# A pre-norm attention block with FP8 linear layer: value projection and input transposes mixed into one bank, an input load issued earlier, and a rearranged last half slot

## What is computed

```python
def attn(x, qkv_w, qkv_b, proj_w, proj_b):          # x: (16, 512, 256), 16 heads of 16
    qkv = einsum('bsd,ed->bse', x, qkv_w) + qkv_b
    q, k, v = per head
    a = softmax(einsum('bhqe,bhke->bhqk', q, k) / 4)
    out = einsum('bhqk,bhke->bhqe', a, v)
    return einsum('bsd,ed->bse', merged(out), proj_w) + proj_b
def ffn(x, w8, bias, input_scale, weight_scale):
    xq = clip(x / input_scale, -448, 448).astype(float8_e4m3fn).astype(x.dtype) * input_scale
    return einsum('bsi,oi->bso', xq, w8 * weight_scale) + bias
x = x + attn(layernorm(x), ...)
x = x + ffn(layernorm(x), ...)
```

## Time and profile before

| | |
|---|---|
| median of the runs | 968.55 us |
| the profiled execution | 968.59 us |
| its span, first to last instruction | 966.8 us |
| PE busy | 930.0 us (96%) |
| DVE busy | 843.8 us (87%) |
| ACT busy | 656.4 us (68%) |
| POOL busy | 515.9 us (53%) |
| one slot in the middle | 55.8 us |

### The profile page before, as it was taken

One profiled execution on the slowest core, in us unless ns is written; L12 is line 12 of the kernel. 1 busy time (PEld: TensorE's weight loads), 2 busy tenths in 40 slices (PEclk: granted clock), 3 DMA queues, 4 the chain that ended last, 5 costly groups with the idle time before them and its releaser, 6 DMA issues.

```text
span 966.8 us, 16811 instructions
## 1 busy us (share of the span) xinstructions
PE 930.0 (96%) x5847; PEld 439.4 (45%) x5847; DVE 843.8 (87%) x1264; ACT 656.4 (68%) x1209; POOL 515.9 (53%) x528
## 2 busy tenths in 40 slices
PE   7799999999999999999999999999999999999993
PEld 4343444444444454544444444444444454433342
DVE  5678889898999989898998989899898989989846
ACT  3157777777777777767677776767777776776760
POOL 4522428467373847647383754738285573715222
PEclk9769999999999999999999999999999999999996
DMA  6971635438083554717265472817556280731010
GB/s 174 159 91 44 107 52 99 79 62 138 29 142 53 100 78 77 124 40 140 44 115 64 83 116 50 140 34 128 72 74 105 35 136 10 136 42 35 13 45 23
DMA packets 46350, 79.45 MB, mean 82 GB/s; under 512 B 10104, under 2 KB 13304, under 8 KB 46264
## 3 DMA queue, kind: packets, MB, share of 16 engines
q1 hardware_dynamic: 45976, 77.97, 47.1%
q10 hardware_dynamic: 288, 0.39, 0.3%
HBM read 18.42 MB, written 8.39 MB: 28 GB/s over the span
## 4 chain that ended last, share of the span: by engine, by line
PE 92%; DVE 2%; ACT 2%; SPq 1%; DMA 1%; issue 1%; ACTq 0%; POOL 0%; DVEq 0%; POOLq 0%
PE ps_t L551 29%; PE ps_o L591 26%; PE ps_m L426 10%; PE ps_s L570 8%; PE ps_m L475 5%; PE ps_m L499 5%; PE ps_m L531 3%; PE ps_m L412 1%; ACT pt L709 1%; PE ps_s L483 1%; DMA xin<-in_x 1%; SPq L309 1%; PE ps_m L514 1%; DVE mx L874 0%; PE ps_s L692 0%
## 5 line engine op out<-in xcount | busy, mean ns | idle before, releaser
L709 ACT ACTIVATE pt<-ps_t 128x512 f32<-128x512 f32 x1024 | 558.0, 598 | 213.9 <-PE ps_t L551 210.5
L874 DVE TENSOR_REDUCE mx<-ps_s 128x2 f32<-128x1024 f32 x512 | 615.3, 1209 | 57.4 <-PE ps_s L570 53.7
L551 PE MATMUL ps_t<-qs,ks 50*128 50x512 f32 x1024 | 391.9, 455 | 8.2 <-ACT pt L709 7.9
L570 PE MATMUL ps_s<-ks,qs 48*128 48x512 f32 x1024 | 380.7, 463 | 8.0 <-DVE nmax L923 4.1
L551 PEld LDWEIGHTS ps_t<-qs,ks 50*128 50x128 f32 x1024 | 164.0, 185 | 296.3 <-ACT pt L709 214.0
L591 PE MATMUL ps_o<-pt,vt 128*32 128x512 f32 x2048 | 272.6, 605 | 0.0
L1176 POOL TENSOR_TENSOR on<-ot,rden 128x256 f32<-128x256 f32 x63 | 39.3, 624 | 243.2 <-DVE rden L935 243.2
L570 PEld LDWEIGHTS ps_s<-ks,qs 48*128 48x128 f32 x1024 | 158.4, 188 | 18.9 <-issue 11.8
L426 PE MATMUL ps_m<-xnT_p,wqkv_p 128*128 128x512 f32 x360 | 109.9, 428 | 1.0 <-POOL xnT_p L1145 1.0
L1167 POOL TENSOR_TENSOR parts<-parts 128x512 f32<-128x512 f32 x60 | 81.3, 1356 | 4.9
L591 PEld LDWEIGHTS ps_o<-pt,vt 128*32 128x32 f32 x2048 | 40.4, 108 | 86.1 <-issue 85.1
(11 more groups left out here) (113 smaller groups left out, 763.3 us busy)
## 6 DMA issues: line engine op xcount, KB each, us to landing
qs<-parts SPq DMA_DIRECT2D x186, 128.0 KB, 4.6
ks<-parts SPq DMA_DIRECT2D x186, 128.0 KB, 5.4
xin<-in_x SPq DMA_DIRECT2D x16, 512.0 KB, 3.6
xres<-in_x SPq DMA_DIRECT2D x16, 512.0 KB, 5.8
out<-h SPq DMA_DIRECT2D x31, 256.0 KB, 2.1
qs<-nmax SPq DMA_DIRECT2D x256, 4.0 KB
pt<-in_qkv_wT SPq DMA_DIRECT2D x1, 768.0 KB, 5.2
qs<-parts SPq DMA_DIRECT2D x12, 64.0 KB, 3.6
```

Source lines behind the costliest of these rows:

```text
L551: nc.tensor.matmul(ps_t[:, g, :], ks[par][rows, slot, keys], qs[par][rows, slot, :], start=True, stop=True).then_inc(st_done, 1)
L570: done = nc.tensor.matmul(ps_s[:, s % 2, g, :], qs[par][rows, slot, queries], ks[par][rows, slot, :], start=True, stop=True)
L709: nc.scalar.activation(pt[n % 2][:, w % 2 + 2 * a, w // 2, :], ps_t[:, a, :], ACT.Exp, scale=SCALE).then_inc(exp_done, 1)
L874: dve.tensor_reduce(mx[:, r, :, s % QUARTER], ps_s[:, s % 2, :, :], AX_X, ALU.max).then_inc(max_done, 1)
```

## The change

1. **Mixed blocks.** `VALUES_AND_X = (20, 22, 24, 26)` takes the place of `PROJECT_V` and `TRANSPOSE_X`. Each of the four steps computes a quarter of the value projection (6 matmuls) into one half of `ps_m` and two x transposes into the other half. ACT makes two copies of 128x256 instead of one of 128x512, four times.
2. **Statistics of x earlier** (`LN1_SUM`, `LN1_END`), and POOL's `layernorm_x` ahead of `low_oT(u-2, 0)`.
3. **Early load**: `load(2, 0)` goes to the head of SP's first slot. The x transposes of block 1 go from slot 1 to the end of PE's first slot, behind 5 unread products; the bias product goes to `ps_m`.
4. **Last half slot**: the transposed scores of odd steps go to `ps_s[:, 0, g, :]`, those of even steps stay in `ps_t`, each waiting for the exponentials of two steps before. Fills shrink from 13 to 4. `round_last` goes from step 8 to 6, `ln2_finish` from 3 to 2, `out_back` from 6 to 5; POOL does `layernorm_h` first.
5. **Finish**: both last `values` come ahead of `project_last(0)`; 10 unread products follow it, 30 more follow the last projection.

```diff
-LAST_ROUND = 8
+LAST_ROUND = 6
+LAST_END = 2
+LAST_BACK = 5
+FILL_VALUES = 10
+FILL_NORM = 30
-FILL_STEPS = range(3, 12)
+FILL_STEPS = (2, 4, 6, 8)
-PROJECT_V = (20, 22)
-TRANSPOSE_X = (24, 26)
-TRANSPOSE_X1 = (0, 2)
+VALUES_AND_X = (20, 22, 24, 26)
-LN1_SUM = (7, 12, 13, 15)
-LN1_END = 17
+LN1_SUM = (5, 7, 10, 12)
+LN1_END = 13
+WARM_SCORES = 5
...
+        def t_bank(b, s, g):
+            if b == B - 1 and s > HALF_STEPS and s % 2:
+                return ps_s[:, 0, g, :]
+            return ps_t[:, g, :]
...
             def first_slot():
+                load(2, 0)
                 sp.wait_ge(ones, 1)
...
                 for n in (2, 3):
                     stack(0, 0, n)
-                load(2, 0)
...
-                for half in range(2):
-                    project_v(0, half)
+                for i in range(NJ):
+                    project_values(ps_t[:, i // 2, i % 2 * D:(i % 2 + 1) * D], 0, i)
+                pe.wait_ge(low_ready, 4)
+                for i in range(WARM_SCORES):
+                    nc.tensor.matmul(ps_s[:, 1, 1, :], wqkv_p[:, 0, 0, 0:P], wqkv_p[:, 0, 0, 0:S], start=True, stop=True)
+                for c in range(NC):
+                    transpose_x(1, c)
...
+            def values_and_x(u, i):
+                take_bank("values_and_x", i, u)
+                project_values(ps_m[:, 0:D], u, i)
+                if u < B - 1:
+                    c, half = i // 2, i % 2
+                    pe.wait_ge(xn_ready, u + 2)
+                    for j in range(2):
+                        last = nc.tensor.transpose(ps_m[:, D + j * P:D + (j + 1) * P],
+                                                   xn[:, 2 * half + j, c * P:(c + 1) * P], ident[:])
+                    last.then_inc(xt_done, 1)
...
+                if b == B - 1 and s == HALF_STEPS + 1:
+                    pe.wait_ge(max_done, STEPS * b + STEPS - 1)
+                elif b == B - 1 and s > HALF_STEPS:
+                    pe.wait_ge(exp_done, 2 * STEPS * b + 2 * s + g - 3)
+                elif past(2 * STEPS * b + 2 * s + g - 1):
                     pe.wait_ge(exp_done, 2 * STEPS * b + 2 * s + g - 1)
...
+            def unread(count):
+                for i in range(count):
+                    nc.tensor.matmul(ps_t[:, 1, :], wqkv_p[:, 0, 0, 0:P], wqkv_p[:, 0, 0, 0:S], start=True, stop=True)
...
             def finish(b):
                 values(b, b % 2, UNITS - 1, 0)
+                values(b, b % 2, UNITS - 1, 1)
                 pe.wait_ge(oT_high, NT * b + 1)
-                pe.wait_ge(nmax_split, 8 * b + 8)
                 project_last(0, PAIRS[0:3:2], False)
-                values(b, b % 2, UNITS - 1, 1)
                 pe.wait_ge(oT_low, NT * b + 1)
                 project_last(0, PAIRS[1:2], False)
+                unread(FILL_VALUES)
                 pe.wait_ge(oT_high, NT * b + 2)
                 project_last(1, PAIRS[0:3:2], False)
                 pe.wait_ge(oT_low, NT * b + 2)
                 project_last(1, PAIRS[1:2], True)
+                unread(FILL_NORM)
...
+            def copy_v(b, par, i):
+                act.wait_ge(v_done, NJ * b + i + 1)
+                if b < B - 1:
+                    act.wait_ge(xt_done, 4 * (b + 1) + i + 1)
                 if past(UNITS * (b - 1)):
                     act.wait_ge(pv_done, UNITS * (b - 1))
...
             def low_xnT(b, c):
-                pool.wait_ge(xnT_ready, 2 * b + c + 1)
+                pool.wait_ge(xnT_ready, 4 * b + 2 * c + 2)
                 if past(b):
-                    pool.wait_ge(v_done, 2 * b)
+                    pool.wait_ge(v_done, NJ * b)
...
             def last_slot(b):
+                layernorm_h(b - 1)
+                out_divide(b, 1)
                 pool.wait_ge(h_ready, 2 * (b - 1) + 2)
                 pool.tensor_tensor(xin[0][:], h[:], b_lin[:].unsqueeze(1).to_broadcast([P, NJ, D]),
                                    ALU.add).then_inc(hb_ready, 1)
-                out_divide(b, 1)
-                layernorm_h(b - 1)
...
+                if present(-1):
+                    layernorm_x(u + 1, 1 - par)
                 if present(2):
                     low_oT(u - 2, 0)
-                if present(-1):
-                    layernorm_x(u + 1, 1 - par)
```

More of the change, by code:

```diff
@@ L708, in exps @@
                 act.wait_ge(st_done, 2 * (STEPS * b + s) + a + 1)
-                nc.scalar.activation(pt[n % 2][:, w % 2 + 2 * a, w // 2, :], ps_t[:, a, :], ACT.Exp, scale=SCALE).then_inc(exp_done, 1)
-            def copy_v(b, par, half):
-                act.wait_ge(v_done, 2 * b + half + 1)
-                if isinstance(b, int) and b == 0:
-                    act.wait_ge(ones, 3)
+                nc.scalar.activation(pt[n % 2][:, w % 2 + 2 * a, w // 2, :], t_bank(b, s, a), ACT.Exp, scale=SCALE).then_inc(exp_done, 1)
@@ L776, in first_slot @@
                 copy_qk(0, 0, 3)
[L777 to L778 removed]
+                copy_first_v(0)
+                copy_first_v(1)
+                for c in range(NC):
+                    copy_xnT(1, c)
             def slot(u, par, present):
```

117 lines of the change are left out of this document (62 added, 55 removed).

## The result

The changed kernel takes **970.37 us**, median of 12 runs (968.16 to 975.75), beside 969.25 us (968.51 to 970.64) for the kernel before in the same comparison. The ratio is 1.0017, 95% interval 1.0009 to 1.0025: 0.17% longer by the medians, less than the 0.2% that the prediction took as the smallest change to be told from none, where 949.4 us (943.5 to 957.5) was forecast. The runs of the changed kernel spread over 7.6 us, those of before over 2.1; the shortest (968.16) has a mean granted clock of 0.983 on PE, the longest (975.75) 0.971. The profiled one is the shortest, span 966.4 us; that of before is 966.8.

A forecast was written before the change was run, and what follows sets the result against it. PE, busy 96% of the span, was taken as the bound. Terms 4.0 (start) + 6.9 (mixed steps) + 1.3 (slot 15) + 6.2 (last half slot) + 0.8 (finish) = 19.2 us from 968.59 gave 949.4 us, range 943.5 to 957.5.

The forecast's parts named there:

- Mixed steps: Slots 1 to 14: steps 20 to 27 fall from 14.30 to 13.81 us, 0.49 a slot, 6.9 us gained.
- the estimate of 0.306: Small ACT copies in mixed steps: skill-based 0.306 us each, leaving ACT 0.19 us of slack instead of 0.26.
- Slot 15: Slot without a next x: steps 20 to 28 fall from 14.29 to 12.97 us, 1.3 us gained.
- the cover of the earlier statistics: Steps 5 to 13: some 0.9 us more DVE work, covered because its maxima run ahead of PE's need.
- The rival that came out: Edits do nothing that counts: DVE becomes the bound, taking back 1.3 us a slot; 967.6 us, chance 0.03.
- slower than before: Rival: ACT late by 0.38 us behind each of four mixed steps, giving 970.7 us; chance 0.04.
- The sign of being wrong that did come: In a middle slot, PE coming to wait for maxima in steps 8 to 15 would show the forecast wrong.
- Last half slot: Two steps take 2.1 us instead of 3.59, last values end at +24.5 instead of +30.7; 6.2 us gained.
- Start: Slot 1: early load and transposes end waits, PE's third projection group starts at 40.5 instead of 43.77; 4.0 us gained.
- the lower bound: Start gains 0 if the transfers only move their queue to the rows of maxima at step 16.
- Finish: Program end: unread products hidden in waits let the linear products run at full clock; 0.8 us gained.
- The rival that it comes up earlier: Slot 1: less idle time may keep PE's clock at 2.4 GHz, about 3 us more, 946.4 us; chance 0.2.

The follow-up runs named there:

- run 1: Changed kernel with only the two tiny DVE operations `nm` and `ve` moved back to step 17; 956.91 us, ratio 0.9875.
- run 5: Changed kernel with the bias addition first on POOL in the last half slot, as in the kernel before; 966.01 us, ratio 0.9965.
- run 6: Changed kernel with the edits of run 1 and run 5 together, and `low_oT(b, 0)` put behind `out_divide(b, 2)`; 953.52 us, ratio 0.9841.
- run 9: run 6 with 31 unread matmuls on PE in the waits of slot 1; 952.56 us, ratio 0.9824.
- run 10: run 8 with POOL's bias addition of the last half slot issued after DVE's rounding instead of first; 952.22 us, ratio 0.9828.
- run 8: run 6 with the rows of maxima ahead of the first stack of slot 1 on SP's queue; 951.94 us, ratio 0.9827.
- run 11: run 10 without the 40 unread matmuls in `finish`; 951.43 us, ratio 0.9832.
- run 4: Changed kernel with `nm` and `ve` left at step 13 but computed by SCALAR_TENSOR_TENSOR, same values; 969.28 us, ratio 1.0001.
- run 7: run 6 without the alternation of banks for transposed scores in the last half slot; 956.58 us, ratio 0.9874.
- run 2: Changed kernel with all statistics late again: sums at steps 7, 12, 13 and 15, end at 17; 961.4 us, ratio 0.9932.
- run 3: Kernel before the change with two unread 128x4 TENSOR_SCALARs added on DVE at step 13; 980.15 us, ratio 1.011.

## Why the prediction was wrong

- **Mixed steps: right.** Steps 20 to 28 of slot 9 take 506.70 to 520.51 = 13.81 us, the very sum; mixed steps take 1.76 to 1.81, odd steps 1.66. ACT kept up: a small copy held it 0.26 to 0.27 us (copies at 508.62 and 508.88, the next exponential at 509.15), the 0.27 that the sum took and not the estimate of 0.306. With the hold gone a slot is 55.33 us against 55.78, a gain of 0.45 for the 0.49 of the term.
- **Slot 15: right.** 54.51 us against 55.76, 1.25 for 1.3.
- **The step that failed** is the cover of the earlier statistics: "where its maxima are ahead of PE's need; if that cover fails, each step late costs PE at most the 0.35 us of a statistic". I summed durations that these operations have beside an idle POOL (0.17 and 0.16) and asked only how much DVE had to do, not what POOL was doing at the new place. At step 17 POOL waits for `ve`; at step 13 it adds the bias for 2.4 us. Two operations then take 1.60 us instead of 0.33, and PE pays 0.9 to 1.0 us in each of 12 slots where at most 0.35 was allowed for: 11.6 us by the slots and 13.5 by the medians. The rival that came out named DVE as the bound in that stretch and gave it 1.3 us a slot and a chance of 0.03; its reason, busy share and more statistics, is not the cause: run 1 keeps them all but for two operations of 0.15 us. That the rival "slower than before" named 970.7, close to the 970.37 measured, is luck: its cause, ACT late behind each mixed step, did not come. The sign of being wrong that did come is PE waiting for maxima, in step 16, one behind the steps that were named.
- **Last half slot: sign right, size wrong.** 2.46 us came for a term of 6.2. I costed `round_last` "as now" and never costed the move of the bias addition on POOL, from before the layer norm of h to beside the rounding. The rounding took 8.5 us and not 6.1. That move cost 2.9 us (run 5: 27.6 to 24.7), half of it the low clock that the traces show behind the longer wait, and a further POOL instruction beside the rounding cost 1.0 (run 6). With both out of the way the last half slot is 6.3 us shorter than before (30.09 to 23.74), the term as forecast, where the clock stays up; in runs 9 and 10 it did not, and 1.5 us of that were lost again. PE's wait before step 10 was put at 2 us; it was 3.75, and 1.35 in run 6.
- **Start: half.** DVE's wait for x went and PE's third projection group starts at 40.60, forecast 40.5. The term of 4.0 measured 2.3 at step 0 of slot 2, which holds the 0.5 of slot 1's own mixed steps too. What took its place was named as the lower bound: the rows of maxima, 2.43 us of waiting at 49.29. Run 8 gets 1.6 to 2.2 of it back by the order of SP's queue.
- **Finish: 0.2 for 0.8.** The eight linear products ran at the full clock (1.21 us). But the ten unread matmuls delay the second half of the projection by 0.8 us (runs 10 and 11), where the prediction had 0.6, "made good" by the clock; the 12 matmuls behind them gained 0.57 (1.59 for 2.16). The term also rests on a clock that the fills don't secure: the same finish, from the last projection to the end, takes 22.25 to 23.28 us in the traces of runs 1 and 4 to 10.
- **The clock in slot 1.** The rival that it comes up earlier didn't come: 0.59 at 40 to 50 us and 0.50 at 50 to 60, and it returns at 62 us in this execution. The moment differs between executions of a slot 1 that is the same but for where or how `nm` and `ve` are computed: in the traces of the changed kernel and of runs 1 and 4 to 7 it is 60 to 62.5 us, with step 0 of slot 2 at 78.16 where the return is at 60 and at 79.3 to 79.8 where it is at 62. In run 2's profile, whose statistics stand elsewhere, it returns at 70, and step 0 of slot 2 comes 3.4 us later than in run 1. So a part of the spread of the runs comes from here; that the changed kernel's 7.6 us and its clocks (0.983 to 0.971) do is argued, since one execution of it has a trace. What sets the moment stays open.

With the POOL effects out of the way the same edits measure 953.52 us (run 6), within the forecast range; the kernel as changed did not get there. What run 6 still lacks to the forecast is for the most part the start: its step 0 of slot 2 comes 2.15 us earlier than before, where 4.5 was forecast for it.

## What to carry to other kernels

An instruction's duration depends on its neighbours as well. When a small DVE operation is moved, or a POOL instruction is moved beside DVE work, read the other engine's timeline at the new place, and price each tiny operation on SBUF of the two forms held here at the time to the end of POOL's current instruction. The operation that is cheapest to do can be the one that holds up a queue. Split a moved step into the part whose result is wanted early (the aggregates) and the part that can be put where POOL is idle (`nm` and `ve`), and test the price with two dummies in the kernel before: run 3, made ahead of the change, would have given it. And a clock that differs between executions of the same code moves single traces by 1 to 3 us: compare stretches of several traces before a small edit is credited with such a sum.
